# First dense block: eight output evictions on ScalarE, and two products and two low halves more on VectorE

## The reference, cut to what matters

```python
# layer 0, after attention: x is 800 x 512 (normalized), Is = 1024, E = 64, TOP_K = 8
gu = x @ shared_gate_up_w                                   # 512 -> 2048
shared = _silu(gu[:, :Is]) * gu[:, Is:] @ shared_down_w     # 1024 -> 512
shared = shared * jax.nn.sigmoid(x @ shared_gate_w)         # one factor per token
probs = jax.nn.softmax(x @ gate_w)                          # 64 experts
w, idx = jax.lax.top_k(probs, TOP_K)
...                                    # place of each (token, expert) pair in its expert's buffer
out_e = _silu(gu_e[..., :I]) * gu_e[..., I:] @ expert_down_w
return y.reshape(T, TOP_K, H).sum(axis=1) + shared
```

## Time and profile before

| | us |
|---|---|
| timed runs, median of 3 | 2391.73 |
| timed runs, lowest and highest | 2384.24, 2392.93 |
| profiled execution | 2411.99 |
| its span, first to last instruction | 2410.2 |
| TensorE busy | 2152.3 (89%) |
| VectorE busy | 1293.2 (54%) |
| ScalarE busy | 1007.2 (42%) |
| POOL busy | 563.1 (23%) |
| granted TensorE clock, mean | 0.946 |

### The profile page before, as it was taken

One profiled execution on the slowest core, in us unless ns is written; L12 is line 12 of the kernel. 1 busy time (PEld: TensorE's weight loads), 2 busy tenths in 40 slices (PEclk: granted clock), 3 DMA queues, 4 the chain that ended last, 5 costly groups with the idle time before them and its releaser, 6 DMA issues. The chain is left out here.

```text
span 2410.2 us, 39542 instructions
## 1 busy us (share of the span) xinstructions
PE 2152.3 (89%) x13422; PEld 1509.6 (63%) x13423; DVE 1293.2 (54%) x2824; ACT 1007.2 (42%) x2099; POOL 563.1 (23%) x556
## 2 busy tenths in 40 slices
PE   5999999977955999999939999999879988999995
PEld 3777777766922444444427777777669436777773
DVE  4677777765513222222256677777651106777776
ACT  2466666653200111111123666666533006566663
POOL 3000000002472455454521000000013202323321
PEclk9999999986987999999969999999969998999997
DMA  7000000003002999999641000000030006766642
GB/s 261 33 31 31 31 31 31 6 1 137 1 1 108 321 305 338 313 339 290 173 161 46 28 28 26 26 26 2 1 137 20 17 34 258 274 209 238 219 178 67
DMA packets 64819, 287.92 MB, mean 119 GB/s; under 512 B 11741, under 2 KB 12143, under 8 KB 45355
## 3 DMA queue, kind: packets, MB, share of 16 engines
q1 hardware_dynamic: 42842, 246.40, 27.2%
q0 software_dynamic: 21840, 39.69, 7.7%
HBM read 257.85 MB, written 33.96 MB: 121 GB/s over the span
## 5 line engine op out<-in xcount | busy, mean ns | idle before, releaser
L661 ACT ACTIVATE probs<-ps,less_max 100x362 f32<-100x362 f32 (+1 forms) x512 | 282.3, 563 | 145.2 <-DVE less_max L537 79.7
L1297 PE MATMUL pgu<-ring,xT 128*128 x560 | 267.4, 600 | 7.9 <-issue 4.3
L647 ACT ACTIVATE pTs<-pt 128x600 f32<-128x600 f32 x256 | 172.5, 674 | 160.4 <-PE pt L439 158.1
L439 PE MATMUL pt<-ident,probs 100*128 100x100 f32 (+1 forms) x1536 | 182.7, 256 | 43.9 <-ACT pTs L647 41.9
L439 PEld LDWEIGHTS pt<-ident,probs 100*128 100x128 f32 (+1 forms) x1536 | 153.2, 141 | 87.0 <-issue 59.5
L571 DVE TENSOR_SCALAR probs<-probs,factor 100x362 f32<-100x362 f32 (+1 forms) x512 | 178.1, 411 | 1.7
L1297 PEld LDWEIGHTS pgu<-ring,xT 128*128 128x128 f32 x560 | 99.7, 191 | 116.7 <-issue 116.5
L1343 ACT ACTIVATE sg<-pgu 128x256 f32<-128x256 f32 x70 | 26.8, 383 | 320.0 <-PE pgu L1297 320.0
L1654 DVE TENSOR_TENSOR ws_low<-w,ws_high 128x2048 fp32r<-128x2048 f32 x63 | 142.9, 2290 | 24.2 <-ACT ws_high L1585 24.2
L942 PE MATMUL pg<-wd,hT 128*100 128x512 f32 x256 | 115.1, 611 | 41.0 <-issue 37.1
L537 DVE CUSTOM_DVE_ANT_0 ps<-ps,madd 100x362 f32<-100x362 f32 (+1 forms) x256 | 128.7, 564 | 24.5 <-PE ps L427 24.3
(11 more groups left out here) (261 smaller groups left out, 5070.2 us busy)
## 6 DMA issues: line engine op xcount, KB each, us to landing
ring<-in_l_ew SPq DMA_DIRECT2D x64, 1536.0 KB
w<-in_l_ew SPq DMA_DIRECT2D x64, 1024.0 KB, 8.2
xnT<-in_ctxT SPq DMA_DIRECT2D x14, 1444.0 KB, 6.6
wu<-in_l_up SPq DMA_DIRECT2D x2, 4096.0 KB, 12.7
b<-in_l_eb SPq DMA_DIRECT2D x8, 1024.0 KB, 4.6
moe_sum<-zrow SPq DMA_DIRECT2D x3, 2048.0 KB, 15.4
moe<-moe_sum SPq DMA_DIRECT2D x24, 200.0 KB
wd<-in_l_down SPq DMA_DIRECT2D x2, 2048.0 KB
```

The lines of the kernel that those rows point to most:

```text
L439: last = pe.transpose(pt[0:n, kc // 3, (kc % 3) * S:(kc % 3 + 1) * S], probs[g % 2 * HPC + j][:, kc * P:kc * P + n], ident[0:S, 0:S])
L647: act.activation(pTs[:, g % 2, j, :, :].rearrange("k (a c) q -> k a (c q)", a=2), pt[:, :, 0:3 * S], ACT.Copy).then_inc(t_out, 1)
L661: act.activation(probs[g % 2 * HPC + j][:, k0:k1], ps[j][0:S, 0:k1 - k0], ACT.Exp, bias=less_max[:, g, seg, j:j + 1], scale=-1.0 if masked ...
L1297: last = pe.matmul(pgu[p][:, :], xT[p][:, c, :], wgu[c], start=c == 0, stop=c == DC - 1)
```

## The change

In layer 0, `BY_POOL` goes from 12 to 10, so products 10 and 11 move from POOL to VectorE. POOL makes the low halves of groups 0 to 5 alone (`LOWS_BY_POOL` = 6); VectorE makes those of groups 6 and 7, ahead of products 10 and 12, and signals them by a semaphore of its own (`w_low_late`). The eight evictions of the down projection move from VectorE to the end of ScalarE's list, as an activation with a scale per token; a new semaphore (`sig_ready`) tells ScalarE that the sigmoids are there, and the wait for the rows of `acc` that SyncE stored (`rows_out`) moves there with them. VectorE's look-ups no longer have an eviction between them. Layer 1 keeps its order.

```diff
--- before.py
+++ after.py
@@ -784,6 +784,7 @@
         xs = [sb(f"xs{part}", [P, DC, T], F32R) for part in ("_high", "_low")]
         ws = [[sb(f"ws{n}{part}", [P, DC, NM, P], F32R) for part in ("_high", "_low")] for n in range(2)]
         x_high, x_low, w_high, w_low = sem("x_high"), sem("x_low"), sem("w_high"), sem("w_low")
+        w_low_late, sig_ready = sem("w_low_late"), sem("sig_ready")
         pl = pb("pl", [P, 2, 512])
         pg, pu = [pb(f"pg{n}", [P, 512]) for n in range(2)], [pb(f"pu{n}", [P, 512]) for n in range(2)]
         ppos, pcnt = pb("ppos", [S, 512]), pb("pcnt", [S, 512])
@@ -811,7 +812,9 @@
         shapes_ready = sem("shapes_ready")
         NP_ = FC * 2
         ROUTE_AT = 6 if swiglu else 12
-        BY_POOL = ROUTE_AT + 6
+
+        BY_POOL = ROUTE_AT + 4
+        LOWS_BY_POOL = BY_POOL // 2 + 1 if swiglu else FC
         NDH = FC // 8
         turned_table = pl[:, 0, 0:2 * (slots // P)].rearrange("p (a n) -> p a n", a=2)
 
@@ -878,7 +881,7 @@
                                            ALU.mult).then_inc(hidden, 1)
                         pool.wait_ge(hidden, n + 1)
                         pool.sem_inc(passed, 1)
-                    if half == 1 and f + 2 < FC:
+                    if half == 1 and f + 2 < LOWS_BY_POOL:
                         split_low(f + 2)
                 pool.wait_ge(table_zero, 16)
                 pool.wait_ge(slots_ready, 2)
@@ -920,7 +923,10 @@
                         last.then_inc(pos_mm, 1)
                     if n >= 2:
                         pe.wait_ge(up_out, n - 1)
-                    pe.wait_ge(w_low, f + 1)
+                    if f < LOWS_BY_POOL:
+                        pe.wait_ge(w_low, f + 1)
+                    else:
+                        pe.wait_ge(w_low_late, f + 1 - LOWS_BY_POOL)
                     for m, dst in enumerate((pg, pu)[:NM]):
                         for c in range(DC):
                             for i, j in PARTS:
@@ -978,6 +984,13 @@
                                        bias=b1[:, f:f + 1]).then_inc(up_out, 1)
                     if half == 1 and f + 2 < FC:
                         split_high(f + 2)
+                if swiglu:
+                    act.wait_ge(sig_ready, 1)
+                    act.wait_ge(env.rows_out, 16 * B)
+                    for t in range(B):
+                        act.wait_ge(down_mm, t + 1)
+                        act.activation(acc[:, t, :], pg[t % 2][0:S, :], ACT.Copy, scale=sig[:, t:t + 1])\
+                            .then_inc(down_out, 1)
 
             @block.vector
             def _(dve):
@@ -1022,6 +1035,7 @@
                 if swiglu:
                     link(dve.tensor_scalar(z[:, :], z[:, :], 1.0, None, ALU.add))
                     link(dve.reciprocal(sig[:, :], z[:, :]))
+                    dve.sem_inc(sig_ready, 1)
                 link(dve.tensor_reduce(red[:, :], logit[:, :, :], AX.X, ALU.add))
                 link(dve.reciprocal(rsum[:, :], red[:, :]))
                 link(dve.tensor_tensor(logit[:, :, :], logit[:, :, :], over_experts(rsum[:, :]), ALU.mult))
@@ -1072,15 +1086,21 @@
                     link(dve.tensor_tensor(posk[:, :, :], posk[:, :, :], behind[:, :, :], ALU.add))
                 dve.tensor_copy(entry[:, :, :, 1], weight[:, :, :]).then_inc(slots_ready, 1)
                 dve.tensor_copy(slot_at[:, :, :], posk[:, :, :]).then_inc(slots_ready, 1)
-                dve.wait_ge(env.rows_out, 16 * B)
                 if swiglu:
                     for n in range(BY_POOL, NP_):
                         f, half = n // 2, n % 2
+                        if half == 0 and f + 1 < FC:
+                            late = f + 1
+                            dve.wait_ge(w_high, late + 1)
+                            dve.tensor_tensor(ws[late % 2][1][:, :, :, :],
+                                              wu_by_chunk[:, :, :, late * P:(late + 1) * P],
+                                              ws[late % 2][0][:, :, :, :].bitcast(F32), ALU.subtract)\
+                                .then_inc(w_low_late, 1)
                         dve.wait_ge(up_out, n + 1)
                         dve.tensor_tensor(hT[:, f, half * TH:(half + 1) * TH], sg[n % 2][:, :], up[n % 2][:, :],
                                           ALU.mult).then_inc(hidden_late, 1)
                 else:
-
+                    dve.wait_ge(env.rows_out, 16 * B)
                     for t in range(B):
                         dve.tensor_tensor(acc[:, t, :], acc[:, t, :], rowb[:, :], ALU.add).then_inc(acc_step, 1)
                     dve.wait_ge(acc_step, B)
@@ -1116,11 +1136,8 @@
                     link(dve.tensor_copy(env.tile_ends[:, 0:E], ends[0:1, :]))
                 for n in range(NDH * B):
                     t = n % B
-                    dve.wait_ge(down_mm, n + 1)
-                    if swiglu:
-                        dve.tensor_scalar(acc[:, t, :], pg[n % 2][0:S, :], sig[:, t:t + 1], None, ALU.mult)\
-                            .then_inc(down_out, 1)
-                    else:
+                    if not swiglu:
+                        dve.wait_ge(down_mm, n + 1)
                         if n == B:
                             dve.wait_ge(down_out, B)
                         dve.tensor_tensor(acc[:, t, :], pg[n % 2][0:S, :], acc[:, t, :], ALU.add)\
```

## The result

| us | timed runs, median (lowest to highest, count) | profiled execution | its span |
|---|---|---|---|
| before | 2388.49 (2380.59 to 2392.93, 6) | 2411.99 | 2410.2 |
| after | 2376.35 (2372.49 to 2380.22, 6) | 2380.22 | 2378.5 |

The changed kernel is 12.1 us faster in the medians; the ratio is 0.995, its 95% interval 0.9931 to 0.9969. The forecast was 2381.7, the range 2355 to 2395. Ratios count the runs within 1.5% of the fastest of their kernel, which leaves out four of e6's twelve and two of e10's; medians and ranges count all.

A forecast was written before the change was run, and what follows sets the result against it. Without late releases the routing table, behind POOL's 64 scatters, bounds the block. Scatters 11.40 us sooner less 1.4 us contention gives 10.0 us: 2391.73 - 10.0 = 2381.7 us, range 2355 to 2395.

The forecast's parts named there:

- What bounds the block: First dense block: ends with the slower of routing table and down projection; without late releases the table, at 743.1 us.
- the late releases of the earlier trace: Down projection: TensorE's finished tiles reached VectorE late, idle up to 37.78 us; somewhat likelier than not absent from timed runs.
- The price of 23.6 us: Block's end in the first profile: what late releases cost that execution, 766.7 - 743.1 us.
- The first scatter, 11.40 us sooner: POOL, after losing two products and two low halves: first scatter at 642.02 us instead of 653.42.
- Contention, +1.4 us: POOL's 64 scatters beside VectorE's two-input operations: more look-ups and products would lengthen them by 1.4 us, bounds 0 to 7.9.
- Rival D: Look-ups in one piece block scatters for whole instructions: gain only 3.5 us, 2388.2 us; chance 0.06.
- The sum: Block's end without late releases: 11.40 - 1.4 = 10.0 us sooner, at 733.1 instead of 743.1.
- ScalarE's evictions at nothing: Down projection: eight evictions moved to ScalarE fit under each tile's 6.87 us, costing zero if the release comes in time.
- The cover, 5.6 us by the forecast: Down projection's end at 725.4 us against the routing table's arrival at 731.0: 5.6 us to spare.
- A: Late releases are in timed runs too and ScalarE is free of them: -33.6 us, 2358.1 us; chance 0.26.
- B: Late releases are in timed runs and hit ScalarE alike: 2391.7 us, down to 2382; chance 0.17.
- C: Timed runs have no late release now, but with ScalarE waiting they get one: +23.6 us, 2415.3 us; chance 0.09.

The follow-up runs named there:

- e6: The changed kernel with product 9 on VectorE too, POOL keeping nine products, on a second chip: 2397.99 us, ratio 0.991 to the kernel before.
- e10: The changed kernel with nine products on POOL, product 9 on VectorE, run again on a third chip: 2391.52 us, ratio 0.9919 to before.
- e1: The kernel before, unchanged, profiled a second time: 2392.6 us in the profile, 2385.64 us timed on that chip.
- e11: The kernel before with POOL's scatters held until the down projection is evicted, on a fourth chip: 2451.08 us, ratio 1.0174.
- e2: The kernel before with only the eight evictions moved to ScalarE: 2387.92 us, ratio 1.0009.
- e3: The kernel before with only POOL's relief, two products and two low halves to VectorE, which still evicts: 2374.16 us, ratio 0.9952.
- e12: The kernel before with each scatter held until the one before has landed, on a fourth chip: 2496.71 us, ratio 1.0356.
- e9: The changed kernel itself, without further edits, on a third chip: 2408.72 us, ratio 1.0013 to the kernel before.
- e5: The changed kernel with the look-ups' second input read from PSUM, on a second chip: 2428.45 us, ratio 1.0057 to the kernel before.
- e4: The kernel before with 16 more scatters, into a spare table, ahead of the 64: 2411.73 us, ratio 1.0108.
- e7: The changed kernel with nine products on POOL, look-ups' second input and VectorE's products' `pu` read from PSUM, second chip: 2422.3 us, ratio 1.0034 to before.

## Why the prediction was right, point by point

**What bounds the block: right.** I judged the late releases of the earlier trace rows "somewhat likelier than not" absent from the timed runs. e1, on a chip where before takes about as long as in the timed runs, shows none. The price of 23.6 us was 20.7 (766.68 against 746.00), or 20.3 by product 9.

**The first scatter, 11.40 us sooner: right**, 13.61 - 2.22 = 11.39. VectorE's slot numbers were ready 1.5 us before product 9 ended, the cover that I named. A 128x1024 low half took 1.23, not 1.15; it hides.

**Contention, +1.4 us: the term that was mis-sized, and in its sign.** The scatters' own loss over 82.26 us fell from 4.98 us (e1: 653.07 to 740.31) to 3.92 (after: 642.97 to 729.15). (Of each sum 0.31 is no contention: e11's scatters, with nothing beside them, take 82.57.) I had counted 0.96 for before from a profile in which late evictions left three look-ups beside scatters. When no release is late, all six lie beside them. The first in e1, on VectorE:

```profile
674.07 1.40 DVE L1089 TENSOR_TENSOR by_tile<-tile_n,ends 1x1216 f32<-1x1216 f32 x1
```

It starts 0.04 us ahead of the scatter of 674.11, which took 2.23. I had also misread the size. 0.28 was not the most that a scatter can lose; it was what was left of the look-up at 693.02 when the scatter of 694.02 came. The rows fit one rule: a scatter that starts beside a VectorE operation with two inputs in SBUF lasts until that operation's end less 0.12, and then its own 0.99. After: 671.25 beside 670.27 + 1.41 gives 0.31 lost, and 685.70 beside 685.64 + 1.33 gives 1.15. Before: 694.02 beside 693.02 + 1.40 gives 0.28. Over all profiles but e11's, where nothing lies beside the scatters, 94 of the 95 scatters that start so fit within 0.03 us. The exception is in the first profile: the scatter of 734.32 started 0.01 us behind a look-up and took 0.98, and the look-up took 1.46. The rule is one half of the exclusion of "Who interferes with whom" ("SBUF — State Buffer", the Trainium skill), which I had set aside as contradicted: the trace agrees with it for a scatter that starts second. The other half does not show: the look-up of 670.27 in the profile after started inside the scatter of 669.96 and took 1.41 like the others. Rival D, drawn from it, still failed, since a scatter that starts first loses nothing, and in one piece of look-ups (one per 2.89 us) two scatters (2 x 1.29 + 0.31 = 2.89) fall in step and lose 0.31 per pair, where look-ups behind an eviction cost 0.4 to 1.2 each. e2 and e3 split the term: with the evictions moved alone the scatters lose 4.16, with POOL's relief alone 4.75, so 0.8 of the 1.06 comes from the evictions' move, which the forecast had as the main source of the cost.

**The sum.** 11.39 + 1.06 - 0.46 (from SyncE's read to the load: 4.91 in place of 4.45) = 11.99 by rows, 12.1 by medians, 10.0 forecast. The block's end, 733.1 forecast, is 734.4 when the execution is moved to start product 9 at 639.81.

**ScalarE's evictions at nothing: right on this chip**, by e2. The cover, 5.6 us by the forecast, was 733.81 - 723.45 = 10.4: by product 9 the transposes came 1.5 us later than forecast and the last eviction 2.9 sooner, for the first eviction of the earlier trace rows, from which I had counted, was itself late (676.58 against e1's 673.40). What I had called a cold first tile was a late release: the eviction came 8.71 us behind TensorE's start, in e1 7.12.

**The rivals.** A did not hold in the timed runs. B and C, the late release that strikes ScalarE too, did not occur there. On three other chips before takes 2413.8, 2408.13 and 2409.12, as it would with late releases; the profiles of two of them show such releases, in other kernels, and the third's show none in e11 and e12. On one of these the changed kernel gains nothing (e9). There the loss starts earlier than I placed it, in the up projection, as the scatters now start beside more of it. Had the timed runs fallen on such a chip, the forecast would have missed by 27 us of 2382 and been outside the range. That they did not is luck that the prediction had priced, at somewhat better than even, and not shown.

## What to carry to other kernels

When one profiled execution lies above the timed runs, take a second profile of the same kernel before any term is sized from it, and repeat a gain of half a per cent on another chip before it is believed. When scatters bound a block, their end is the first start plus 1.29 us for each, plus what they lose beside VectorE; place the two-input VectorE operations so that they begin behind a scatter and not ahead of one. The evictions' move was not needed on e1's chip; e3, with POOL's relief alone, gained as much (0.9952 against 0.995).

## What the runs showed of the hardware

- The release of a TensorE result came late by up to some 50 us: ScalarE idle for 54.50 us in e5, where 3.5 are usual. It struck VectorE and ScalarE (e5 to e10) alike, and with the early scatters it began in the up projection. It was seen beside back-to-back scatters of 100 pairs each, one per 1.29 us, and not beside one per 3.0 us (e12) nor without any (e11). On e1's chip the same scatters did no harm in four profiles (e1 to e4). Which part of the chip holds the signal stays open: the rows name no releaser.
- A scatter waits out a VectorE operation with two SBUF inputs that started before it, all but 0.12 us (94 of 95 within 0.03); the VectorE operation grew by 0.06 at most (a look-up of 1.46 us at 734.31 in the first profile). Beside an operation with one SBUF input it takes its 0.99: the TENSOR_REDUCE behind each look-up (0.98 for the scatter of 676.64 in e1), and a product with its second input in PSUM (e7).
- The landing of a scatter came some 2.0 us behind POOL's end of it (60 of e12's 63 waits are 1.97 to 2.05, the longest 3.76).
- Nine products beat before on the two chips whose profiles show late releases (0.991 and 0.9919), and the changed kernel on the one of them where it was run (1.0013). On a chip without them it was not timed. There it could win 1.6 us at most from an earlier start: its first scatter follows the slot numbers by 1.03 us (e6: 637.79 behind 636.76), after's by 2.65. Of this, e6's second scatter lost 0.92 again beside a low half.
- Left open: whether the changed kernel with its evictions on VectorE (e3) keeps its gain on a chip with late releases; it ran only on e1's chip.
